# GpSimd's order of scatters, row gathers and gathers of t at the first pair of a chunk, in a one-core LoRA and block-diagonal FFN kernel

## What is computed

```
y   = einsum('bsi,boi->bso', x, weight[ids])          # LoRA stage
t   = y[:, perm]                                      # 1024 features, shuffled
t   = t.reshape(tokens, 16 heads, 64)
t   = einsum('bhd,hdm->bhm', t, up)                   # 64 -> 256 in each head
t   = gelu(t)
t   = einsum('bhm,hmd->bhd', t, down)                 # 256 -> 64 in each head
out = x + t[:, argsort(perm)]
```

## Time and profile before

| | |
|---|---|
| median of three runs | 309.11 us (308.97 to 309.88) |
| the profiled execution's own time | 309.95 us |
| its span, first to last instruction | 308.1 us |
| TensorE busy | 296.6 us, 96% |
| VectorE, ScalarE, GpSimd busy | 177.8, 159.0, 109.3 us |
| mean granted TensorE clock | 0.987 of full speed |
| moved by DMA | 77.87 MB, mean 253 GB/s |

### The profile page before, as it was taken

The page is one execution under the profiler, slowest core; times in us unless marked ns, Lnnn a source line. Parts: engine busy times, 40 slices in busy tenths (PEclk is TensorE's granted clock), DMA queues, the critical chain, the costliest instruction groups (busy, mean ns, idle before and its releaser), DMA issues.

```text
span 308.1 us, 4315 instructions
## 1 busy us (share of the span) xinstructions
PE 296.6 (96%) x1672; PEld 212.5 (69%) x1672; DVE 177.8 (58%) x210; ACT 159.0 (52%) x179; POOL 109.3 (35%) x104
## 2 busy tenths in 40 slices
PE   8999999999999999999999999999985999999994
PEld 3888888888878587685867768586763684554441
DVE  2779769679748674656548563684613722434332
ACT  4645533554658633828256362845325306677750
POOL 2000000078430271552608062112770573755234
PEclk9999999999999999999999999999995999999999
DMA  6999999999997785698747877661673174545213
GB/s 197 350 423 419 421 417 382 341 297 401 405 362 271 262 323 222 215 332 306 264 168 254 305 275 272 199 210 49 203 230 103 68 226 151 186 157 165 75 68 136
DMA packets 23779, 77.87 MB, mean 253 GB/s; under 512 B 2896, under 2 KB 11472, under 8 KB 18768
## 3 DMA queue, kind: packets, MB, share of 16 engines
q1 hardware_dynamic: 6912, 43.39, 38.0%
q0 software_dynamic: 7712, 25.18, 23.8%
q10 hardware_dynamic: 9136, 9.05, 8.4%
HBM read 60.82 MB, written 16.78 MB: 252 GB/s over the span
## 4 chain that ended last, share of the span: by engine, by line
PE 93%; another core or an unknown queue 3%; DVE 1%; issue 1%; POOL 1%; ACT 0%; POOLq 0%; DVEq 0%; ACTq 0%
PE ps L513 36%; PE ps L562 18%; PE ps L514 18%; PE ps L541 6%; PE ps L547 5%; PE ps L544 5%; PE ps L482 3%; PE ps L473 2%; PE ps L487 1%; DVE y_out L407 1%; POOL out_rows L267 1%; ACT hidden L329 0%; DVE w_raw L416 0%; DVE rows L430 0%
## 5 line engine op out<-in xcount | busy, mean ns | idle before, releaser
L513 PE MATMUL ps<-x_pair,w_hi 128*128 128x512 f32 x480 | 171.2, 401 | 0.0
L514 PE MATMUL ps<-x_pair,w_lo 128*128 128x256 f32 x480 | 134.8, 281 | 0.0
L513 PEld LDWEIGHTS ps<-x_pair,w_hi 128*128 128x128 f32 x480 | 90.2, 188 | 29.0 <-issue 6.8
L329 ACT ACTIVATE hidden<-ps 128x1024 f32<-128x1024 f32 x64 | 61.0, 1030 | 71.3 <-PE ps L547 57.4
L295 ACT ACTIVATE w_hi<-w_raw 128x1024 fp32r<-128x1024 f32 x60 | 60.4, 1060 | 60.4 <-PE ps L514 32.2
L514 PEld LDWEIGHTS ps<-x_pair,w_lo 128*128 128x128 f32 x480 | 90.7, 189 | 0.0
L383 DVE TENSOR_TENSOR w_lo<-w_raw,w_hi 128x1024 fp32r<-128x1024 f32 x60 | 70.7, 1219 | 13.6 <-ACT w_hi L295 13.6
L407 DVE TENSOR_REDUCE y_out<-ps 128x256 f32<-128x512 f32 x64 | 42.7, 686 | 46.4 <-PE ps L514 33.0
L250 POOL DMA_INDIRECT t_raw<-y_rows,idx x32 | 33.1, 1033 | 99.0 <-DMA y_rows<-y_out 82.8
L562 PE MATMUL ps<-hidden,down_sb 128*64 128x512 f32 x256 | 58.9, 604 | 0.7 <-ACT hidden L329 0.7
L562 PEld LDWEIGHTS ps<-hidden,down_sb 128*64 128x64 f32 x256 | 17.2, 138 | 34.8 <-issue 33.1
(11 more groups left out here) (26 smaller groups left out, 122.7 us busy)
## 6 DMA issues: line engine op xcount, KB each, us to landing
w_raw<-w SPq DMA_DIRECT2D x30, 1024.0 KB
y_rows<-y_out ACTq DMA_DIRECT2D x32, 256.0 KB
x_raw<-x_cols SPq DMA_DIRECT2D x7, 1024.0 KB
w_raw<-w SPq DMA_DIRECT2D x4, 256.0 KB, 5.3
hidden<-up SPq DMA_DIRECT2D x1, 1024.0 KB, 10.5
down_sb<-down SPq DMA_DIRECT2D x1, 1024.0 KB, 10.7
w_raw<-w SPq DMA_DIRECT2D x2, 384.0 KB, 6.8
x_raw<-x_cols ACTq DMA_DIRECT2D x2, 256.0 KB, 3.5
```

The costliest lines, as they stand in the source:

```text
L329: nc.scalar.activation(hidden[:, f % HS, m, :, :], up_banks(f, m)[:, :, :], ACT.Gelu).then_inc(gelu_done, 1)
L513: nc.tensor.matmul(acc, w_hi[:, ws, k, col], x_pair[:, xs, k, :, :], start=(k == 0), stop=False)
L514: last = nc.tensor.matmul(acc[:, 0, :], w_lo[:, ws, k, col], x_hi[:, xs, k, :], start=False, stop=(k == KT - 1))
```

## The change

In three of the passes of GpSimd's loop, p = 2, 6 and 10, where f = 2p+4 is 8, 16 and 24, the first of a chunk, the two `gather_t` are issued behind the scatters and the row gathers of the same pass, and not ahead of them. Pass -2 (f = 0) is left out by `p > 0`; in pass 14 f is 32 and there is nothing to gather. The late row gathers of pass 10 (f = 28 to 31) stay in front of everything.

```
                 if 2 * p + 4 == NF - FU:
                     for f in LAST_ROWS:
                         gather_late_rows(f)
+
+                new_chunk = (2 * p + 4) % FU == 0 and p > 0
                 for f in (2 * p + 4, 2 * p + 5):
-                    if f < NF:
+                    if f < NF and not new_chunk:
                         gather_t(f)
                 for f in (2 * p - 4, 2 * p - 3):
                     if 0 <= f:
                         scatter(f)
                 for f in (2 * p + 3, 2 * p + 4):
                     if 0 <= f < LATE:
                         gather_rows(f)
+                for f in (2 * p + 4, 2 * p + 5):
+                    if f < NF and new_chunk:
+                        gather_t(f)
                 for f in LATE_ROWS.get(p, ()):
                     gather_late_rows(f)
```

## The result

The changed kernel takes **314.51 us** as the median of six runs (311.46 to 318.18), the kernel before on the same chip 309.8 us (six runs, 308.97 to 311.38). The ratio is 1.0098, with a 95% interval of 1.0055 to 1.0142; the two medians themselves are 4.7 us or 1.5% apart, a little more than the interval allows. The change is slower by 1 to 1.5%, outside the predicted range of 307.7 to 310.6 and on the side that had a chance of 0.13. The execution that was profiled is the shortest of the six: its own time is 311.46 us, its span 309.6 us, against 309.95 and 308.1 before. It shows where the time is lost, but less of it than the median.

The account below looks back on a forecast made before the run. TensorE, busy 96% of the span, was taken to bound the kernel. Passes 2, 6 and 10 cost 0 each on the profiled 309.95 us; as a median of runs the forecast was 309.1 us, range 307.7 to 310.6.

Parts of the forecast that it names:

- the side that had a chance of 0.13: Whole kernel slower than 309.1 us by more than 0.93 us; chance 0.13.
- Where the issues go: GpSimd's queue: t8 issued near 114.5, t16 near 186, t24 near 264.6, with scatter 16 at 262.0.
- bounds of 4.6 and 6.3: Landing time in us of a t gather, taken from two trace rows of gathers of the same shape.
- Passes 2 and 6, 0 us each: t8 and t16 go later but are read some 30 us after their new issue; cost 0 each.
- t24 in time: Pass 10: t24 lands at 269.2, 1.3 us ahead of ScalarE, 3.2 ahead of what TensorE can bear.
- Pass 10, 0 us: t24 issued 5.55 us later, behind scatters 16 and 17; GpSimd back at old times by scatter 20; cost 0.
- that rival: Behind pass 10: ten unbroken issues hold back TensorE's word of products; up to 6.8 us, 315.9 us; chance 0.08.
- the prediction's own sign of being wrong: A new TensorE wait for `t_lo` or gelu between 268 and 282; other signs were clock or group 14 changes.
- The 2.38 us that it named: GpSimd's pause among the issues of pass 10, named with one of 0.86 us, to become unbroken issue, 262.0 to 274.8.
- the stretch of group 14: Group 14 takes 24.80 us against group 13's 18.00, mean clock 0.86; the only stretch taken as slow.
- Three runs within 0.9 us say that the stall is a steady one: Argument against group 14's stall going away with the change, a case given 0.06.
- The faster rival: Group 14's stall goes away as GpSimd's queue history changes: 6.8 us less, 302.3 us; chance 0.06.

Follow-up runs that it names:

- the spread kernel: Late row gathers 28 to 31 moved to passes 14 and 15, two GpSimd pauses added, against the kernel before: 0.9996 on chip 6, 0.9712 on chip 9.
- pass 10 alone: t24 and t25 put behind scatters 16 and 17, passes 2 and 6 as in the kernel before: 315.21 us against 310.58, ratio 1.0142.
- spare scatters: Kernel before plus 14 unneeded scatters ending pass 5: 2 KB rows 1.0014 on chip 6, 1.0393 on chip 3; 64 B rows 1.0023 on chip 6.
- the kernel with scatters 12 and 13 moved: Kernel before with scatters 12 and 13 taken from pass 8 to pass 9, ahead of scatter 14: 310.72 us against 310.81, ratio 1.0003.

## Why the prediction was wrong

- **Where the issues go: right.** Scatter 16 and t24 stand 2.60 us apart; t8 is issued at 113.64, 114.5 named, and t16 at 184.60, 186 named. The median landing of a gather of t, which the trace of before did not give, is 5.1 us in the spread kernel on number 6 and between 4.8 and 5.6 us in the others there, inside the bounds of 4.6 and 6.3. The fit of the Trainium skill (DMA: Bandwidth & Descriptors, anatomy of one DMA on the gpsimd path), 2.6 us for these 256 KB, is too small for this kernel by about half.
- **Passes 2 and 6, 0 us each: right.** Alone they give 1.0003.
- **t24 in time: right.** `t_high` has 0.0 us of idle time, and on number 6 the order by itself costs nothing (301.7 us without it, 302.1 with it).
- **Pass 10, 0 us: wrong.** It costs what the sum left to a rival. The sum asked only whether the moved transfers land in time; it put the closing up of GpSimd's short pauses at nothing. In the trace those of 0.75 and 0.86 us are gone and TensorE waits 0.80 and 1.53 us for it, the prediction's own sign of being wrong ("a wait of TensorE for `t_lo` or for gelu between 268 and 282"). The 2.38 us that it named beside the 0.86 were not closed up. With pass 10 alone the loss is 4.6 us, 1.42%.
- **The step that failed is the argument against that rival**: "the kernel has the stretch of group 14 as the only slow one, while passes 2 and 6 also have runs of eight or seven issues with scatters in the middle, at full pace". It is true and says nothing on ten. In the traces from the chips with the hold, a stretch of eight issues was on time (105.6 to 116.7 in the kernel before), and those of nine and more in the late part were not. The trace of before held the case between, nine issues from 242.6 to 254.9. Beside them, up(18) and its gelu, and an undisturbed pair of the same kind, on TensorE and on ScalarE:

```profile
252.97 0.50 PE L541 MATMUL ps<-t_hi,up_hi 64*128 64x512 f32 x2
...
267.58 0.50 PE L541 MATMUL ps<-t_hi,up_hi 64*128 64x512 f32 x2
```

```profile
255.60 1.94 ACT L329 ACTIVATE hidden<-ps 128x1024 f32<-128x1024 f32 x2 [14.30 <-PE ps L547]
...
268.64 1.94 ACT L329 ACTIVATE hidden<-ps 128x1024 f32<-128x1024 f32 x2 [2.51 <-PE ps L547]
```

From the up matmuls to the gelu it is 2.63 us in the first and 1.06 us in the second: word was 1.6 us late. The prediction did not use it, and it speaks for a stretch of ten more than passes 2 and 6 speak against it.
- **The price: nearer than its chance.** The rival named 6.8 us and 315.9 us. The medians lie above the kernel before by 4.7 us on the first chip, 4.6 with pass 10 alone, 6.7 on number 3 and 4.0 on number 9; the ratios say 1.0 to 1.7%, 3 to 5 us. On number 3 a second hold adds to it (last section). The 6.8 us held half a clock for a while, and the clock does count in some executions. Where only the wait came, in the profiled execution of the changed kernel, the pair lost 2.9 us. With pass 10 alone it took 285.85 - 274.89 = 10.96 us and lost 4.4, with the clock at its lower level for a part of it. The 10 us from up(25) on, first with pass 10 alone, then in the changed kernel, and the starts of the pair and of the next with pass 10 alone:

```profile
279.10:289.10 10.00, 9.97 (x54) 5.53 (x56) 2.77 (x4) 5.35 (x8) 5.84 (x6) 0.83 0.44 153
276.90:286.90 10.00, 9.93 (x62) 5.16 (x64) 3.37 (x5) 6.80 (x10) 6.23 (x6) 1.00 0.45 157
```

```profile
274.89 0.50 PE L546 MATMUL ps<-t_hi,up_hi 64*128 64x512 f32 x2
...
285.85 0.50 PE L546 MATMUL ps<-t_hi,up_hi 64*128 64x512 f32 x2
```
- **"Three runs within 0.9 us say that the stall is a steady one": wrong.** It is steady on the chips 3, 9 and 11 and on the first, and absent on number 6. The faster rival's 302.3 us for a group 14 without its stall is close to what the spread kernel reaches, 301.5.

## What to carry to other kernels

A move that costs nothing by its transfers can still close the pauses of the queue it stands in: count the issues in a row and the pauses between them before and after, not only when each lands; here two of 0.75 and 0.86 us were what the move took away. When an engine that waits for TensorE shows a releaser that the profile does not know, look at what GpSimd was doing in the 10 us before, and look for smaller delays of the kind elsewhere in the same trace. And a loss on one chip is to be tried on a second one, before it is called the kernel's.

## What was not expected of the hardware

The word of a finished product came late by up to 4.2 us in the changed kernel and by far more with spare scatters (a wait of 12.72 us), while TensorE itself went on; with the spare scatters it too stood still five times beside it, for 0.6 to 1.7 us. On chips 3, 9 and 11 this came with stretches of nine or more indexed transfers issued some 1.28 us apart, and ended within some 2.7 us of the stretch's end. Number of issues and length in time are not told apart by these runs, nor is the number of issues from the bytes that they move. One stretch of before, 62.4 to 78.9, had 11 issues and was on time; its issues are slower, 1.5 us each, beside VectorE's work. In the profiled execution of the changed kernel on number 3 the same place had 15 issues, and was held: VectorE at 89.52 waited 4.32 us, and TensorE 2.10 us behind it. And the kernel with scatters 12 and 13 moved was held a little with six issues, a pause of 0.63 us and four more. So the threshold is not a clean one.

What the mechanism is stays open, and so does whether it belongs to the chip or to the recording of its executions, since every run here was recorded. On the chips with the hold the pages give no landing times for the gathers of t, on number 6 they do; but the spread kernel on number 9 has none either, and no hold. The Trainium skill (NOTIFIC — the notification-queue block, the section on overflow) says that the path of the records, when it is full, can in one of its three settings stall the engine that writes to it; no run here shows whether that happened. An execution without any record was not tried, and the changed kernel without the spreading was not run on number 6.
